# Moving one value step between two places of a software pipeline, with a new order of key and value projections, in a fused attention block

## The reference, cut to what matters

```
qkv = w_qkv @ x                     # 1536 x 1024; 8 heads of 64 for q, k, v
sim = (q * 1/8).T @ k               # per head, 1024 x 1024
out = softmax(sim) @ v
y   = w_out @ out + b_out
y   = y * rsqrt(mean(y*y, channels) + 1/8) * rms_scale
result = y + x
```

## Time and profile before

| | us |
|---|---|
| median of 3 runs (3929.11 to 3931.4) | 3930.39 |
| the profiled execution's own time | 3928.97 |
| its span in the trace | 3926.7 |
| PE matmuls busy | 3890.7 (99%) |
| POOL, DVE, ACT busy | 2961.6, 2765.4, 2316.0 |

### The profile page before, as it was taken

The page is one execution under the profiler, slowest core; times in us unless marked ns, Lnnn a source line. Parts: engine busy times, 40 slices in busy tenths (PEclk is TensorE's granted clock), DMA queues, the critical chain, the costliest instruction groups (busy, mean ns, idle before and its releaser), DMA issues.

```text
span 3926.7 us, 53756 instructions
## 1 busy us (share of the span) xinstructions
PE 3890.7 (99%) x18650; PEld 2470.0 (63%) x18650; DVE 2765.4 (70%) x2897; ACT 2316.0 (59%) x4057; POOL 2961.6 (75%) x2335
## 2 busy tenths in 40 slices
PE   8999999999999999999999999999999999999998
PEld 5666666666666666666666666666666666666664
DVE  5667676676766777667676776767767676676766
ACT  4556565565655656556565665756657565565564
POOL 6678777787876868777787777877778777787776
PEclk9999999999999999999999999999999999999999
DMA  4111111111111112112021120110201111111110
GB/s 151 48 50 54 44 65 54 44 54 44 68 52 43 64 34 71 49 44 76 22 73 53 37 76 33 65 54 36 73 33 65 54 38 70 45 53 54 38 60 22
DMA packets 71851, 212.24 MB, mean 54 GB/s; under 512 B 8216, under 2 KB 9368, under 8 KB 58784
## 3 DMA queue, kind: packets, MB, share of 16 engines
q1 hardware_dynamic: 71584, 208.80, 15.0%
HBM read 168.92 MB, written 39.85 MB: 53 GB/s over the span
## 4 chain that ended last, share of the span: by engine, by line
PE 94%; DVE 4%; issue 1%; ACT 0%; POOL 0%; DMA 0%; DVEq 0%; POOLq 0%
PE pv L763 24%; PE aux L584 16%; PE score L741 13%; PE score L750 11%; PE aux L628 9%; PE aux L657 8%; PE aux L726 7%; PE pv L682 3%; PE aux L707 2%; DVE inv_sum L1183 1%; DVE k_l L1118 1%; DVE maxima L1125 1%; DVE aux L1131 0%; DVE y_sb L1196 0%; PE aux L642 0%
## 5 line engine op out<-in xcount | busy, mean ns | idle before, releaser
L1306 POOL TENSOR_TENSOR prob_sum<-prob_sum,probs 128x512 f32<-128x512 f32 x1536 | 1953.2, 1301 | 354.7 <-ACT probs L871 354.7
L871 ACT ACTIVATE probs<-score 128x512 f32<-128x512 f32 x2048 | 1111.6, 596 | 786.1 <-PE score L750 779.6
L1125 DVE TENSOR_REDUCE maxima<-aux 128x1 fp32r<-128x1024 f32 x768 | 913.5, 1217 | 357.8 <-PE aux L726 210.0
L763 PE MATMUL pv<-probs,v_sb 128*64 128x512 f32 x4096 | 977.7, 603 | 0.0
L741 PE MATMUL score<-q_hl,k_hh 128*128 128x512 f32 x2048 | 839.5, 410 | 2.3 <-ACT probs L871 2.3
L750 PE MATMUL score<-q_hm,k_l 72*128 72x512 f32 x2048 | 814.4, 398 | 0.5 <-DVE q_hm L1143 0.5
L584 PE MATMUL aux<-x_hi,w_ring 128*128 128x512 f32 x2048 | 656.0, 398 | 7.9 <-DVE x_lo L374 7.1
L1302 POOL TENSOR_TENSOR prob_sum<-probs 128x512 f32<-128x512 f32 x256 | 324.9, 1291 | 356.8 <-ACT probs L871 354.7
L763 PEld LDWEIGHTS pv<-probs,v_sb 128*64 128x64 f32 x4096 | 254.1, 136 | 489.6 <-issue 463.4
L741 PEld LDWEIGHTS score<-q_hl,k_hh 128*128 128x128 f32 x2048 | 387.4, 189 | 167.0 <-issue 90.6
L584 PEld LDWEIGHTS aux<-x_hi,w_ring 128*128 128x128 f32 x2048 | 387.7, 190 | 97.6 <-DVE w_ring L1205 7.0
(11 more groups left out here) (132 smaller groups left out, 5099.9 us busy)
## 6 DMA issues: line engine op xcount, KB each, us to landing
w_ring<-w_split SPq DMA_DIRECT2D x93, 1024.0 KB, 4.8
stage<-x SPq DMA_DIRECT2D x252, 256.0 KB, 5.2
out<-stage SPq DMA_DIRECT2D x124, 256.0 KB, 2.0
w_split<-w_ring SPq DMA_DIRECT2D x3, 1024.0 KB, 11.8
w_split<-y_sb SPq DMA_DIRECT2D x3, 1024.0 KB, 3.9
y_sb<-wqkv SPq DMA_DIRECT2D x4, 512.0 KB, 8.5
probs<-wqkv SPq DMA_DIRECT2D x2, 512.0 KB, 7.3
probs<-wout SPq DMA_DIRECT2D x1, 1024.0 KB, 8.3
```

The lines of the kernel that those rows point to most:

```text
L763: pe.matmul(pv[half][e * D:(e + 1) * D, :], v_sb[:, pair // 2, j, (pair % 2) * P + e * D:(pair % 2) * P + (e + 1) * D], probs[:, (b * SLOT ...
L871: act.activation(probs[:, step % RING, e, :], score[e][:], ACT.Exp, scale=SOFT).then_inc(prob_ready, 1)
L1125: dve.tensor_reduce(maxima[:, n:n + 1], bank(k, 2), AX_X, ALU.max).then_inc(aux_free[k], 1)
L1306: pool.tensor_tensor(prob_sum[:, e, :], prob_sum[:, e, :], probs[:, step % RING, e, :], ALU.add).then_inc(prob_added, 1)
```

## The change

Five groups of edits:

1. Value step 4 moves from place 1 of the next slot to place 9 of its own: place 9 has steps 0 to 4 (`EARLY_VALUES = 5`), place 1 has step 5, tile 0, steps 6, 7, sums, tile 1.
2. `VALUES_FIRST` goes from (2, 1, 0, 0, 0, 1, 2, 0) to (0, 1, 1, 0, 1, 1, 0, 0): tile 2 leads place 9 in slots 0 and 6 and comes after one value step in slots 2 and 4.
3. Slot 0: K1 whole at place 5 (it was halved over 5 and 7), the mean R from place 3 to 7, and the high part of the normalised output on ACT from place 4 to 8.
4. Slot 6: K0 at place 3, K1 at 5, V1 at 7 in bank 3 (it was V1, K0, K1).
5. ACT in slot 5 repeats the queries before it splits pieces 0 to 3 of x, not after. In the prologue DVE casts the mask and the identity before tile 3, not tile 1.

```diff
-OUTPUT_HIGH_AT = (4, 8, 8, 4, 8, 6, 4, 4)
+OUTPUT_HIGH_AT = (8, 8, 8, 4, 8, 6, 4, 4)
+EARLY_VALUES = 5
-VALUES_FIRST = (2, 1, 0, 0, 0, 1, 2, 0)
+VALUES_FIRST = (0, 1, 1, 0, 1, 1, 0, 0)
-MEAN_AT = ((0, 3), (1, 7))
+MEAN_AT = ((0, 7), (1, 7))
@@ items_at
-    if t == 3 and slot in (0, 2, 4):
+    if t == 3 and (slot in (0, 2, 4) or slot == 6 and projected):
         out.append(("K0", 0))
-    elif t == 3 and (slot in (1, 3) or slot == 6 and projected or slot == 7 and following):
-        out.append(({1: "V0", 3: "V2", 6: "V1", 7: "V2"}[slot], 0))
-    if t == 5 and slot == 6 and projected:
-        out.append(("K0", 1))
-    elif t == 5 and slot in (2, 4):
+    elif t == 3 and (slot in (1, 3) or slot == 7 and following):
+        out.append(({1: "V0", 3: "V2", 7: "V2"}[slot], 0))
+    if t == 5 and (slot in (0, 2, 4) or slot == 6 and projected):
         out.append(("K1", 1))
     if t == 7:
-        if slot == 0:
-            out.append(("K1", 1))
-        elif slot in (1, 3):
+        if slot in (1, 3):
             out.append((f"V{slot}", 1 if slot == 1 else 3))
         elif slot == 6 and projected:
-            out.append(("K1", 2))
+            out.append(("V1", 3))
@@ in_halves
-    return name == {0: "K1", 1: "V1", 3: "V3", 5: "V0", 7: "V3"}.get(slot)
+    return name == {1: "V1", 3: "V3", 5: "V0", 7: "V3"}.get(slot)
@@ PE, place 1
                             if preceding:
-                                values(before[0], before[1], 4, before[2])
                                 values(before[0], before[1], 5, before[2])
@@ PE, place 9
-                            for j in range(STEPS // 2):
+                            for j in range(EARLY_VALUES):
@@ PE, place 13 of the very last slot
-                                values(body, slot, 4, False)
                                 values(body, slot, 5, False)
@@ ACT, place 0
-                        if t == 0 and slot in (5, 6) and not body.last:
-                            for c in range(2 * KT):
-                                if (slot, t) == SPLIT_HIGH_AT[c] and (slot == 5 or c < 6):
-                                    split_x(c, body.b + 1)
+                        if t == 0 and slot == 6 and not body.last:
+                            for c in (4, 5):
+                                split_x(c, body.b + 1)
...
                             repeat_queries(body, slot)
-                        if t == 0 and slot == 6 and not body.last:
-                            for c in (6, 7):
+                        if t == 0 and slot in (5, 6) and not body.last:
+                            for c in range(4) if slot == 5 else (6, 7):
                                 split_x(c, body.b + 1)
@@ DVE, prologue
-                elif (slot, name) == (7, "M10"):
+                elif (slot, name) == (7, "M30"):
```

## The result

The kernel after takes 4085.99 us in the median of 4 runs (4084.08 to 4088.49) against 3930.68 us before: ratio 1.0396, 95% interval 1.0378 to 1.0414. That is 155 us slower where 123 were forecast. It is 33 us above the forecast of 4053 and 10 us above the stated range.

The account below looks back on a forecast made before the run. PE's own stream, busy 99%, was taken as the bound. 3928.97 + 47.4 + 60 + 25.5 - 15 + 4 + 0.5 = 4051.4, so 4053 us with the median 1.4 higher; 8-in-10 range 4015 to 4076.

Parts of the forecast that it names:

- The moved value step costs nothing by itself: Places 1 and 9: place 1 loses 0.86 us and place 9 gains 0.86 in every slot, net 0.
- 4 x 0.43 of the text: Slot 0: time of the four value steps still ahead, said to be more than ACT's two exponentials need.
- Tile 0, +47: Place 1: tile 0 comes before Q's bank is released, waiting 0.30 or 0.50 us, 126 times: 47.4 us.
- Slot 6, +60: Slot 6, place 5: K1 waits 4.0 us for DVE's low part of piece 6, in 15 bodies.
- The clock, +25.5: Behind slot 6's stand: PE's clock falls once per body for 3.4 us, costing 1.7 us, 15 times.
- Two such stretches: Rival, 10%: the clock stays low for two 3.4 us stretches per slot 6 stand, giving 4078 us.
- Place 9, -15 and +4: Place 9: four old stalls go, -15 us; one new stall in slot 0 adds 4 us.
- The new wait of slot 0: Slot 0: tile 2's second head waits 0.28 us for DVE to release R's bank, 15 times: +4 us.
- The faster rival: Rival, 3%: DVE's releases come before PE needs them, only place 9's stalls count, giving 3919 us.

Follow-up runs that it names:

- e4: Kernel before with only value step 4 moved to place 9, VALUES_FIRST and slots 0 and 6 as before: 3979.66 us, ratio 1.0129.
- e1: Kernel after with DVE's low part of piece 6 of x at place 1 of slot 6, not place 4: 3982.55 us, ratio 1.0136.
- e5: Kernel before with only slot 6's new order (K0, K1, V1 at places 3, 5, 7): 4033.18 us, ratio 1.0264.
- e2: Kernel after with piece 6 of x at place 2 of slot 6, between `o_norm` and K0's subtractions: 4059.43 us, ratio 1.0332.
- e6: Kernel before with slot 0's change alone (K1 whole at place 5, R at 7, output's high part at 8): 3944.28 us, ratio 1.0036.

## Why the prediction fell short, step by step

The 155 us by the distances in the trace of after: slot 6's stand 15 x 4.31 = 65; the slow K1 14 x (5.25 - 2.77) + 1.64 = 36; tile 0 49; slot 0's scores 12, and 2 more in the first body (its slot 0 takes 30.77 us against 28.99); slot 1's tile 2 4; place 9's old waits -14. Together 154; 1 us is not assigned.

- **The moved value step costs nothing by itself:** right. Five steps take as much more as the one less gives back, and the waits alone give 3978 for e4, 2 us from what it took. Four value steps take 4 x 0.86 us, not the 4 x 0.43 of the text; the slip was on the safe side.
- **Tile 0, +47:** right in cause and size: 0.31 us in the slots with Q in the first bank, 0.51 in the others by the distances, 49 us; e4 gave +50 in all.
- **Slot 6, +60:** right in place, order and releaser (e1, e5), 5 us too low: line 373 took 1.01 us there, not the 0.68 of the earlier trace rows. It took 0.80 in e1 and 1.20 in e2; what sets that isn't known.
- **The clock, +25.5:** this is the step that failed. That the clock would fall at every stand was right; the size of the fall was not. I took one low stretch of 3.4 us per stand, 1.7 us, from the earlier trace rows. The low clock lasted 6.8 us in 14 of the 15 bodies, of which K1 filled 5.25, and it cost 2.48 us each; only the first body was as forecast, 3.4 us and 1.64. Two such stretches stood as a rival at 10%, at 4078 us. It had the length right and the price too high, 3.4 us per stand where 2.48 came, because the low clock began while PE still stood. The Trainium skill's section "HAM oscillation — how this bites in real kernels" ("TensorE: Matmul & The Clock Gate") says that waits between bursts put the clock down anew each time, and the kernel after agrees: it fell in 15 of 15 bodies. e2 shows that the stand's size doesn't settle the length.
- **Place 9, -15 and +4:** all four old waits went, 14 us. The new wait of slot 0 was put on the wrong step: I tested whether DVE would release R's bank, and not whether ACT would have the exponential of place 6 ready. That one came first and was 0.8 us, and it then hid the wait for R's bank. +12 instead of +4, and 2 more in the first body, which has no R and was not looked at (e6: +14 in all).
- **Slot 1's tile 2:** missed, 4 us. PE reaches place 9 0.5 us sooner, and DVE's chain, which hangs on the slot's start, doesn't move. It is the argument that I made for tile 0, not carried on to the next waits.
- **The faster rival** falls at the point named: Q's release was at 2.28 us after the scores.

The clock (+11), slot 0 (+8, and 2 in the first body), slot 6 (+5), slot 1 (+4) and tile 0 (+2) make up 32 of the 33 us that were missing. So the clock is the largest miss, and a third of the whole. The range was at fault too: it ended at 4076, below the rival of 4078 that had 10%, and it left out most of the bounds given term by term (tile 0 up to 63, slot 6 up to 69, the clock up to 51, slot 0 up to 15). All these terms came out within them; only slot 1's 4 us and the first body's 2 had none.

## What to carry to other kernels

When a saturated engine is made to reach a wait earlier, ask for each later wait whether its releaser hangs on that engine's stream or on something that doesn't move; a change of the order must be laid beside every other engine's program order, here one subtraction that came to stand behind K0's two. When an idle time is predicted for TensorE, give the low clock behind it a range of its own, since its length varied here with the same idle time, and carry the bounds of the terms into the range of the sum. A wait booked as "issue" is found by what ended just before it on the other engines.

## What the runs showed of the hardware

- A single stand of PE of 4.3 us with busy neighbours lowered the granted clock to 1.2 GHz each time in the kernel after and in e5, 15 of 15 bodies in both; one of 3.1 us (e2) still did in 13 of 15 bodies, for a mean clock of 0.67 and 0.80 over the same piece of work in turn.
- In slot 6 the low clock lasted 6.8 us in all 36 bodies where it fell while PE still stood, and 3.4 us in all 7 where it fell after K1 had begun (kernel after, e2, e5).
- In body 6 of the kernel after the clock fell while PE still stood (1748.84, with K1 at 1750.29) and stayed low through 5.25 us of dense matmuls.
- The same DVE subtraction of 128x512 took 0.68 us (before), 0.80 (e1), 1.01 (after, e5) and 1.20 (e2) at four places of the order; the cause is open.
